# Expert layers of a transformer-like kernel: four of 32 token tiles taken unsorted through all eight experts

## The chip, the cores and the metric

The kernel runs on one core of one Trainium2 chip, in one launch. The metric is the device time in microseconds; lower is better. Engines are TensorE (PE, with its weight loads as PEld), VectorE (DVE), ScalarE (ACT), GpSimd (POOL) and SyncE (SP), which here only starts DMAs.

## The reference, cut to what matters

The input is 4 x 1024 tokens of 128 numbers, float32. Four layers follow each other, each as x = x + layer(layernorm(x)): an attention, a mixture of experts, a delta-rule attention, and the mixture of experts again. The change touches the two expert layers alone, which use the same weights:

```python
x = hidden_states.reshape(-1, H)                 # 4096 rows of 128
probs = softmax(x @ gate_w)                      # 8 experts
top_w, top_i = top_k(probs, 2)
top_w = top_w / sum(top_w)
route = zeros((m, E)); route[row, top_i] = top_w
for e in range(E):                               # 8 experts, F = 256
    h = silu(x @ w1[e]) * (x @ w3[e])            # 128 -> 256, twice
    out = out + route[:, e:e+1] * (h @ w2[e])    # 256 -> 128
```

A row thus needs two of the eight experts.

## The kernel before

All of x lies in on-chip memory as 32 tiles (`NT`) of 128 rows; the weights of all experts lie in `wall` (`all_w_all` in the trace). `moe` is one expert layer; it is called twice ("moe1", whose output the next layer norm reads, and "moe2", whose output is the kernel's). Each engine has its own instruction list, and they meet at semaphores; nothing is reordered by a scheduler. A layer has four stages.

**Planning.** VectorE finds the two best experts of each row (`find_best`), marks the row's pair of experts among 28 (`PAIRS`; `count_pairs` writes `member` and its sum `chosen`), and TensorE sums `chosen` over lanes (`before`, `total`, semaphore `s_pos`). From these, `pair_totals` works out where each pair begins; `experts_of_tiles` works out which experts each sorted tile needs; `places` gives each row its slot in the sorted order (`slot`); `order_passes` and `read_plan` turn it into a list of passes, which the engines later read into registers. ScalarE meanwhile writes the normalised rows into `xr`, with the row's weights behind them.

**Scatter.** When `slot` is there, GpSimd starts one indirect DMA per tile, 32 in all, which write the rows of `xr` to DRAM in sorted order (`expert_rows`). When all have landed, SyncE loads the sorted tiles back (`moe_moe_xs`).

**Passes.** Sorted by pairs, a tile needs few experts. There are `NPASS` = 2 * 32 + 27 = 91 passes of one tile through one expert. A pass is `up` (four 128x128 products into `ps_up`, weights from a copy `wbuf` that ScalarE makes), Silu on ScalarE, `product` on VectorE, `down` (two products into `ps_y`) and `add` on VectorE. TensorE runs `up(n)` and then `down(n - 2)`, and turns a sorted tile every second pass (`turn_rows`, into `ps_g`; VectorE copies it to `xgT`).

**Return.** For each sorted tile whose passes are done, GpSimd starts an indirect DMA that adds the tile's rows to the copy of x in DRAM (`rows_and_out` in moe1, the output itself in moe2). In moe1 SyncE then loads x back in four pieces, and VectorE takes each tile's statistics (`bn_stats_of`) for the next layer norm.

A float32 product of 128 moving columns or of 512 stands in the trace as two records, a turned tile as one.

## Time and profile before

| | us |
|---|---|
| median of 3 runs | 1899.91 (1897.85 to 1900.02) |
| the profiled execution | 1899.49 |
| its span, first to last instruction | 1897.8 |
| mean granted TensorE clock, share of full speed | 0.824 |
| moe1, from its first instruction to the last statistics | 863.8 to 1074.4 |
| moe2, from its first instruction to the end | 1694.9 to 1897.8 |

Starts are counted from the first instruction of the span. "PEclk" is the granted clock in a stretch as a share of full speed: 0.50 is 1.2 GHz and 1.00 is 2.4 GHz. The two expert layers are 413 us of the span. Over the whole span PE is busy 67% of the time and DVE 76%, but these are means over stages with different limits, so what matters here is read from the stages of one expert layer.

### The profile page before, as it was taken

Reading aid. Unit: us, or ns where it says so; the run is one execution under the profiler, and the core shown is the slowest. Engines: PE = TensorE matmul, PEld = TensorE weight load, DVE = VectorE, ACT = ScalarE, POOL = GpSimd, SP = SyncE. Lnnn points to the kernel's source line nnn. Section 1 sums busy time; section 2 is a strip of 40 time slices with the busy share of each in tenths; the row PEclk is TensorE's granted clock in tenths of the full one; section 3 lists DMA queues with packets and bytes.
Section 4 is the critical chain, followed back from the end, with each engine's and each line's share of the span. In section 5 each row is a group of like instructions: output and inputs, shape, how many; then the busy total and the mean of one; then the engine's idle time right before and its main releaser. Section 6 shows DMA issues by size and latency. Waiting matters only on the chain. (4 is left out here: it accounts for less than half of the span.)

```text
span 1897.8 us, 41781 instructions
## 1 busy us (share of the span) xinstructions
PE 1272.3 (67%) x15730; PEld 780.1 (41%) x15730; DVE 1438.5 (76%) x2659; ACT 963.9 (51%) x2025; POOL 327.9 (17%) x408
## 2 busy tenths in 40 slices
PE   4689999999999999992499483000000039950998
PEld 2214555555555555452499342000000014430997
DVE  4698989999989999515265485999999979871564
ACT  4607888888888888874266372000222200021565
POOL 6100000000000000004325200000000025546055
PEclk9859999999999999995699785555555569985999
DMA  3520111111111110022312326810222110011222
GB/s 94 171 55 9 41 42 32 31 31 31 31 31 31 31 31 3 3 67 64 82 12 26 56 94 125 208 45 11 52 54 63 40 50 0 1 45 48 54 23 25
DMA packets 100857, 92.14 MB, mean 49 GB/s; under 512 B 20977, under 2 KB 82226, under 8 KB 100274
## 3 DMA queue, kind: packets, MB, share of 16 engines
q1 hardware_dynamic: 83778, 76.08, 15.4%
q0 software_dynamic: 11264, 8.92, 3.3%
q10 hardware_dynamic: 5616, 4.47, 1.4%
q8 instruction: 127, 2.08, 0.5%
q14 instruction: 72, 0.59, 0.1%
HBM read 47.28 MB, written 31.21 MB: 41 GB/s over the span
## 5 line engine op out<-in xcount | busy, mean ns | idle before, releaser
L727 DVE TENSOR_REDUCE att_negmax<-att_ps_max 128x1 f32<-128x1024 f32 x512 | 621.0, 1224 | 66.7 <-PE att_ps_max L590 38.0
L715 ACT ACTIVATE att_probs<-att_ps_prob 128x512 f32<-128x512 f32 x1024 | 556.4, 595 | 129.4 <-PE att_ps_prob L605 127.2
L590 PE MATMUL att_ps_max<-av_k_op,av_q_op 81*32 81x512 bf16 x4096 | 423.1, 401 | 13.2 <-PEq L104 7.2
L605 PE MATMUL att_ps_prob<-av_q_op,av_k_op 99*32 99x512 bf16 x4096 | 412.3, 382 | 2.8
L625 PE MATMUL att_ps_acc<-att_probs,att_vq 128*32 128x256 f32 x4096 | 317.7, 379 | 0.0
L1960 PE MATMUL out_ps_y<-all_bo_row,all_ones 1*128 1x128 f32 x2 | 0.8, 481 | 372.7 <-PEq L104 372.7
L1123 PE MATMUL moe_moe_ps_up<-moe_moe_xgT,moe_moe_wbuf 128*128 x1456 | 196.6, 279 | 0.0
L1123 PEld LDWEIGHTS moe_moe_ps_up<-moe_moe_xgT,moe_moe_wbuf 128*128 128x128 f32 x1456 | 181.4, 196 | 0.1
L590 PEld LDWEIGHTS att_ps_max<-av_k_op,av_q_op 81*32 81x32 bf16 x4096 | 117.0, 97 | 142.6 <-DVE att_negmax L727 44.7
L605 PEld LDWEIGHTS att_ps_prob<-av_q_op,av_k_op 99*32 99x32 bf16 x4096 | 108.8, 95 | 146.2 <-ACT att_probs L715 88.7
L625 PEld LDWEIGHTS att_ps_acc<-att_probs,att_vq 128*32 128x32 f32 x4096 | 135.5, 111 | 75.6 <-issue 1.0
L1181 ACT ACTIVATE moe_moe_gate<-moe_moe_ps_up 128x256 f32<-128x256 f32 x182 | 70.0, 385 | 165.9 <-PE moe_moe_ps_up L1123 159.0
L1960 PEld LDWEIGHTS out_ps_y<-all_bo_row,all_ones 1*128 1x128 f32 x2 | 0.5, 304 | 372.9 <-issue 372.9
L1862 ACT ACTIVATE solve_p<-solve_state,solve_decay 128x32 f32<-128x32 f32 x128 | 45.0, 352 | 155.6 <-DVE solve_state L1846 155.6
L1173 ACT ACTIVATE moe_moe_wbuf<-all_w_all 128x512 f32 x182 | 113.3, 622 | 14.5 <-issue 14.4
L1131 PE MATMUL moe_moe_ps_y<-all_w_all,moe_moe_hT 128*128 x728 | 111.5, 276 | 1.3 <-DVE moe_moe_y L1337 1.3
L1337 DVE SCALAR_TENSOR_TENSOR moe_moe_y<-moe_moe_ps_y,moe_moe_xs,moe_moe_y 128x128 f32 x182 | 63.9, 351 | 62.8 <-issue 60.4
L1328 DVE TENSOR_TENSOR moe_moe_hT<-moe_moe_gate,moe_moe_ps_up 128x256 f32<-128x256 f32 x182 | 76.7, 421 | 43.2 <-PE moe_moe_ps_y L1131 31.8
L531 POOL CAST att_nm_parts<-att_nm_rows 32x128 bf16<-32x128 f32 x16 | 4.6, 286 | 547.2 <-ACT att_nm_rows L696 547.2
L1131 PEld LDWEIGHTS moe_moe_ps_y<-all_w_all,moe_moe_hT 128*128 128x128 f32 x728 | 96.1, 192 | 2.1 <-issue 2.1
L1955 POOL TENSOR_TENSOR out_qS<-b_q,out_St 128x1024 f32<-128x1024 f32 x32 | 75.4, 2355 | 65.8 <-DVE out_St L2064 65.8
L1323 DVE COPY moe_moe_xgT<-moe_moe_ps_g 128x128 f32<-128x128 f32 x64 | 18.2, 284 | 82.0 <-issue 80.7
(276 smaller groups left out, 1737.2 us busy)
## 6 DMA issues: line engine op xcount, KB each, us to landing
av_k_op<-terms_k SPq DMA_DIRECT2D x48, 216.0 KB
av_q_op<-terms_q SPq DMA_DIRECT2D x144, 72.0 KB
solve_dec_and_windows<-solve_Xw SPq DMA_DIRECT2D x16, 256.0 KB, 3.0
solve_dec_and_windows<-solve_k SPq DMA_DIRECT2D x16, 256.0 KB, 3.7
moe_moe_xs<-expert_rows SPq DMA_DIRECT2D x6, 576.0 KB, 6.6
terms_q<-qkv_parts_q SPq DMA_DIRECT2D x8, 384.0 KB, 2.6
terms_k<-qkv_parts_k SPq DMA_DIRECT2D x8, 384.0 KB, 3.1
all_w_all<-in_f_w SPq DMA_DIRECT2D x24, 128.0 KB, 2.4
```

Source lines behind the costliest of these rows:

```text
L590: mm = pe.matmul(ps_max[c * STRIP:(c + 1) * STRIP, a % 2, k * CH:(k + 1) * CH], q_op[s][0:R_ALL, h, at:at + STRIP], k_op[s][0:R_ALL, h, k ...
L605: mm = pe.matmul(ps_prob[c * STRIP:(c + 1) * STRIP, j % 2, :], k_op[s][0:R_END, h, at:at + STRIP], q_op[s][0:R_END, h, half * CH:(half + 1 ...
L625: mm = pe.matmul(ps_acc[half][32 * h:32 * h + 32, cols], vq[:, s % 2, kt, VW * h:VW * h + 32], probs[:, (GH * v + h) % PROBS, cols], start ...
L715: act.activation(probs[:, j % PROBS, :], ps_prob[:, j % 2, :], ACT.Exp).then_inc(s_exp, 1)
L727: dve.tensor_reduce(negmax[:, s % 2, a:a + 1], ps_max[:, a % 2, :], AX.X, ALU.max, negate=True).then_inc(s_maxed, 1)
L1123: mm = pe.matmul(ps_up[n % 3][:, i * P:(i + 1) * P], wbuf[:, n % 3, i * P:(i + 1) * P], xgT[:, bass.ds(row, P)], start=True, stop=True)
L1131: mm = pe.matmul(ps_y[n % 2][:, 0:P], hT[:, n % 3, i * P:(i + 1) * P], wall[:, bass.ds(at0 + (2 * F + i * P), P)], start=(i == 0), stop=(i ...
L1173: act.activation(wbuf[:, n % 3, :], wall[:, bass.ds(at0, 2 * F)], ACT.Copy).then_inc(s_wb, 1)
L1181: act.activation(gate[:, n % 3, :], ps_up[n % 3][:, 0:F], ACT.Silu).then_inc(s_silu, 1)
L1328: dve.tensor_tensor(hT[:, n % 3, :], gate[:, n % 3, :], ps_up[n % 3][:, F:2 * F], ALU.mult).then_inc(s_h, 1)
L1337: dve.scalar_tensor_tensor(out=tile, in0=ps_y[n % 2][:, 0:P], scalar=xs_flat[:, bass.ds(col, 1)], in1=tile, op0=ALU.mult, op1=ALU.add).the ...
L1955: pool.tensor_tensor(qS[:, e % 2, :], q[:, b * S:(b + 1) * S], St[:, e % 2, :], ALU.mult).then_inc(s_qS, 1)
```

## The change

The first four tiles of x (`ND`, 512 rows) are no longer sorted, scattered and returned. TensorE turns them to `xdT`, and they go through all eight experts as they lie, 512 rows at a time: for each expert `first_up` twice (two products of 512 columns each, into four `ps_up` banks), `first_silu`, `first_product`, `first_down` (eight products of 128 columns) and `first_sum`, which adds the weighted result into `y_d`. A weight of zero makes an expert that a row doesn't need drop out. This work stands in the instruction lists between the planning steps and ahead of the passes. The other 28 tiles (`NS`) are sorted as before, so that there are 28 scatters, 2 * 28 + 27 = 83 passes and 28 returns. `places` stands ahead of `experts_of_tiles`. ScalarE's normalisations are spread between the Silus, and each scatter waits for its own tile's piece (`PIECE`, four tiles) instead of for all. In moe1 the DRAM copy of x is laid out with the 32 rows of a lane behind each other, so that a lane's share of a load or store is one run; it comes back in pieces of seven tiles instead of eight. In moe2 SyncE stores the four tiles by itself.

```diff
-NPASS = 2 * NT + PAIRS - 1
+ND = 4
+NS = NT - ND
+NPASS = 2 * NS + PAIRS - 1
 COL_W, COL_ID, COL_ZERO, ROW = P, P + E, P + 12, 144
 PIECE = 4
 NPIECE = NT // PIECE
-PARTS = [0, 1, 2, 4, 8, 16, 24, 32]
-BACK = 8
+PARTS = [0, 1, 2, 4, 8, 16, 22, NS]
+BACK = 7
...
+        xdT = m.sb("xdT", [P, CH])
+        gate_d = m.sb("gate_d", [P, 2, CH])
+        hT_d = m.sb("hT_d", [P, 2, MF, CH])
+        y_d = m.sb("y_d", [P, ND, P])
...
-        ps_up = [m.ps(f"ps_up{i}", [P, 2 * F]) for i in range(3)]
+        ps_up = [m.ps(f"ps_up{i}", [P, 2 * F]) for i in range(4)]
...
-        resid_tiles = resid.rearrange("(t p) c -> p t c", p=P)
-        landed = 16 * NT * (layer + 1)
+        resid_tiles = resid.rearrange("(p t) c -> p t c" if out is None else "(t p) c -> p t c", p=P)
+        per_tile, per_lane = (1, NT) if out is None else (P, 1)
+        landed = 16 * NS * (layer + 1)
...
-            sp.dma_start(resid_tiles, g.x[:, :, :]).then_inc(s_kept, 16)
+            sp.dma_start(resid_tiles[:, ND:, :], g.x[:, ND:, :]).then_inc(s_kept, 16)
...
+            if not norm_next:
+                sp.wait_ge(s_dadd, 1)
+                sp.dma_start(resid_tiles[:, 0:ND, :], g.x[:, 0:ND, :]).then_inc(s_dout, 16)
...
+                for i in range(NS // BACK):
+                    some = slice(ND + i * BACK, ND + (i + 1) * BACK)
...
+            pool.iota(xr[:, :, COL_ID:COL_ID + 1].bitcast(mybir.dt.int32), pattern=[[per_tile, NT], [0, 1]],
+                      base=0, channel_multiplier=per_lane).then_inc(s_ids, 1)
...
-            pool.wait_ge(s_xn, NPIECE)
             pool.wait_ge(s_weight, 1)
             pool.wait_ge(s_slot, 1)
-            for t in range(NT):
-                pool.indirect_dma_start(scr.xg, bass.IndirectOffsetOnAxis(slot[:, t:t + 1], 0), xr[:, t, :],
+            for t in range(NS):
+                pool.wait_ge(s_xn, (ND + t) // PIECE + 1)
+                pool.indirect_dma_start(scr.xg, bass.IndirectOffsetOnAxis(slot[:, t:t + 1], 0), xr[:, ND + t, :],
                                         None).then_inc(s_scat, 16)
...
+            def first_up(u):
+                e, i = u // MF, u % MF
+                wait_used(pe, s_dh, u - 1)
+                for half in range(2):
+                    at0 = e * WE + half * F + i * P
+                    mm = pe.matmul(ps_up[(2 * u + half) % 4][:, :], wall[:, at0:at0 + P], xdT[:, :],
+                                   start=True, stop=True)
+                mm.then_inc(s_dup, 1)
+
+            def first_down(e):
+                pe.wait_ge(s_dh, MF * (e + 1))
+                wait_used(pe, s_dsum, e - 1)
+                for t in range(ND):
+                    for i in range(MF):
+                        at0 = e * WE + 2 * F + i * P
+                        mm = pe.matmul(ps_y[e % 2][:, t * P:(t + 1) * P], hT_d[:, e % 2, i, t * P:(t + 1) * P],
+                                       wall[:, at0:at0 + P], start=(i == 0), stop=(i == MF - 1))
+                mm.then_inc(s_dy, 1)
+
+            pe.wait_ge(s_xn, 1)
+            for t in range(ND):
+                mm = pe.transpose(ps_g[:, t * P:(t + 1) * P], xr[:, t, 0:P], g.ident[:, :])
+            mm.then_inc(s_dturn, 1)
+            pe.wait_ge(g.s_experts, 16 * 3 * E)
+            pe.wait_ge(s_dT, 1)
+            first_up(0)
+            first_up(1)
             pe.wait_ge(s_earlier, 2)
             pe.wait_ge(s_chosen, 1)
             pe.matmul(before, earlier[:, :], chosen[:, :], start=True, stop=True)
             pe.matmul(total, g.ones[:, :], chosen[:, :], start=True, stop=True).then_inc(s_pos, 1)
-            pe.wait_ge(s_count, 1)
-            pe.matmul(ps_prefix, earlier[:, :], local[:, E - 1:E], start=True, stop=True).then_inc(s_prefix, 1)
-            pe.wait_ge(s_turns, 1)
-            pe.wait_ge(s_tables, 9)
-            for e in range(E):
-                pe.matmul(ps_row, tile_b[:, :], turn_of[:, e, :], start=(e == 0), stop=(e == E - 1))
-            for e in range(E):
-                mm = pe.matmul(ps_exp, exp_b[:, e:e + 1], turn_of[:, e, :], start=(e == 0), stop=(e == E - 1))
-            mm.then_inc(s_passes, 1)
+            for e in range(1, E):
+                first_up(2 * e)
+                first_up(2 * e + 1)
+                first_down(e - 1)
+                if e == 1:
+                    pe.wait_ge(s_count, 1)
+                    pe.matmul(ps_prefix, earlier[:, :], local[:, E - 1:E], start=True, stop=True).then_inc(s_prefix, 1)
+                if e == 2:
+                    pe.wait_ge(s_turns, 1)
+                    pe.wait_ge(s_tables, 9)
+                    for j in range(E):
+                        pe.matmul(ps_row, tile_b[:, :], turn_of[:, j, :], start=(j == 0), stop=(j == E - 1))
+                    for j in range(E):
+                        mm = pe.matmul(ps_exp, exp_b[:, j:j + 1], turn_of[:, j, :], start=(j == 0), stop=(j == E - 1))
+                    mm.then_inc(s_passes, 1)
+            first_down(E - 1)
...
+                if n == 0:
+                    pe.wait_ge(s_dsum, E)
...
+            def normalise(q):
                 for tile in range(q * PIECE, (q + 1) * PIECE):
                     op = act.activation(xr[:, tile, 0:P], g.x[:, tile, :], ACT.Identity,
                                         bias=g.nmr[:, tile:tile + 1], scale=g.rstd[:, tile:tile + 1])
                 op.then_inc(s_xn, 1)
-                if q == 2:
-                    act.wait_ge(s_gap, 1)
-                    act.activation(tanh[:, :, :], gap[:, :, :], ACT.Tanh, scale=0.5).then_inc(s_tanh, 1)
+
+            def first_silu(e):
+                for u in (2 * e, 2 * e + 1):
+                    act.wait_ge(s_dup, u + 1)
+                    wait_used(act, s_dh, u - 1)
+                    act.activation(gate_d[:, u % 2, :], ps_up[2 * u % 4][:, :], ACT.Silu).then_inc(s_dsilu, 1)
+
+            normalise(0)
+            normalise(1)
+            act.wait_ge(s_dturn, 1)
+            act.activation(xdT[:, :], ps_g[:, :], ACT.Copy).then_inc(s_dT, 1)
+            normalise(2)
+            act.wait_ge(s_gap, 1)
+            act.activation(tanh[:, :, :], gap[:, :, :], ACT.Tanh, scale=0.5).then_inc(s_tanh, 1)
+            first_silu(0)
+            normalise(3)
+            normalise(4)
+            for e in range(1, E):
+                first_silu(e)
+                if 4 + e < NPIECE:
+                    normalise(4 + e)
...
+            places()
+
+            def first_product(u):
+                dve.wait_ge(s_dsilu, u + 1)
+                wait_used(dve, s_dy, u // MF - 1)
+                dve.tensor_tensor(hT_d[:, u // MF % 2, u % MF, :], gate_d[:, u % 2, :],
+                                  ps_up[(2 * u + 1) % 4][:, :], ALU.mult).then_inc(s_dh, 1)
+
+            def first_sum(e):
+                dve.wait_ge(s_dy, e + 1)
+                wait_used(dve, s_dsum, e)
+                for t in range(ND):
+                    weight = xr[:, t, COL_W + e:COL_W + e + 1]
+                    part_y = ps_y[e % 2][:, t * P:(t + 1) * P]
+                    if e == 0:
+                        op = dve.tensor_scalar(y_d[:, t, :], part_y, weight, None, ALU.mult)
+                    else:
+                        op = dve.scalar_tensor_tensor(out=y_d[:, t, :], in0=part_y, scalar=weight, in1=y_d[:, t, :],
+                                                      op0=ALU.mult, op1=ALU.add)
+                op.then_inc(s_dsum, 1)
+
+            first_product(0)
+            first_product(1)
             experts_of_tiles()
-            places()
-            order_passes()
-            read_plan()
+            dve.wait_ge(s_weight, 1)
+            for e in range(1, E):
+                first_product(2 * e)
+                first_product(2 * e + 1)
+                first_sum(e - 1)
+                if e == 1:
+                    order_passes()
+                if e == 3:
+                    read_plan()
+            first_sum(E - 1)
+            dve.wait_ge(s_dsum, E)
+            dve.wait_ge(s_xn, 1)
+            dve.tensor_tensor(g.x[:, 0:ND, :], g.x[:, 0:ND, :], y_d[:, :, :], ALU.add).then_inc(s_dadd, 1)
+            if norm_next:
+                dve.wait_ge(s_dadd, 1)
+                for t in range(ND):
+                    bn_stats_of(nc, g, t)
...
-                for i in range(NT // BACK):
+                for i in range(NS // BACK):
                     dve.wait_ge(s_home[i], 16)
-                    for t in range(i * BACK, (i + 1) * BACK):
+                    for t in range(ND + i * BACK, ND + (i + 1) * BACK):
```

TensorE's list at the start of moe1 (`ps_p` holds the planning's small products, `ps_g` the turned tiles) was this before, up to the first pass:

```order
L1102 MATMUL moe_moe_ps_p<-moe_moe_chosen,moe_moe_earlier 128x28
L1103 MATMUL moe_moe_ps_p<-moe_moe_chosen,all_ones 128x28
L1105 MATMUL moe_moe_ps_p<-moe_moe_local,moe_moe_earlier 128x1
L1109 MATMUL moe_moe_ps_p<-moe_moe_turn_of,moe_moe_tile_b 1x128 x8
L1111 MATMUL moe_moe_ps_p<-moe_moe_turn_of,moe_moe_exp_b 1x128 x8
L891 TENSOR_LOAD moe_moe_pe_at
L1116 MATMUL moe_moe_ps_g<-all_ident,moe_moe_xs 128x128 x2
L1123 ISA
L1123 MATMUL moe_moe_ps_up<-moe_moe_xgT,moe_moe_wbuf 128x128 x4
```

With the change the same place begins so (L1126 is `first_up`, L1136 `first_down`):

```order
L1142 MATMUL moe_moe_ps_g<-all_ident,moe_moe_xr 128x128 x4
L1126 MATMUL moe_moe_ps_up<-moe_moe_xdT,all_w_all 128x512 x4
L1150 MATMUL moe_moe_ps_p<-moe_moe_chosen,moe_moe_earlier 128x28
L1151 MATMUL moe_moe_ps_p<-moe_moe_chosen,all_ones 128x28
L1126 MATMUL moe_moe_ps_up<-moe_moe_xdT,all_w_all 128x512 x4
L1136 MATMUL moe_moe_ps_y<-all_w_all,moe_moe_hT_d 128x128 x8
L1158 MATMUL moe_moe_ps_p<-moe_moe_local,moe_moe_earlier 128x1
L1126 MATMUL moe_moe_ps_up<-moe_moe_xdT,all_w_all 128x512 x4
L1136 MATMUL moe_moe_ps_y<-all_w_all,moe_moe_hT_d 128x128 x8
L1163 MATMUL moe_moe_ps_p<-moe_moe_turn_of,moe_moe_tile_b 1x128 x8
```

Four products of 512 columns and their turns now stand ahead of the two sums over `chosen` on which the slots depend, and the remaining planning products stand between the experts. Thirty-two products of 512 columns and 64 of 128 stand ahead of the first `TENSOR_LOAD` of a pass.

VectorE's list from `chosen` on was this before (`place` to `slot` are `places`, `upper` to `local` are `experts_of_tiles`):

```order
L1247 TENSOR_REDUCE moe_moe_chosen<-moe_moe_member 128x28
...
L1262 TENSOR_TENSOR moe_moe_member<-moe_moe_base,moe_moe_ps_p 128x28
L1266 TENSOR_SCALAR moe_moe_upper<-moe_moe_ends,moe_moe_tile_to 128x28
...
L1273 SCALAR_TENSOR_TENSOR moe_moe_local<-moe_moe_unit,moe_moe_needed 128x8
L1278 SCALAR_TENSOR_TENSOR moe_moe_place<-moe_moe_carry,moe_moe_member 128x924
L1282 TENSOR_TENSOR moe_moe_picked<-moe_moe_member,moe_moe_place 128x896
L1283 TENSOR_REDUCE moe_moe_slot_f<-moe_moe_picked 128x32
L1284 TENSOR_SCALAR moe_moe_slot<-moe_moe_slot_f 128x32
```

and is this now; the last rows are what stands between the last expert and the first sorted tile:

```order
L1353 SCALAR_TENSOR_TENSOR moe_moe_place<-moe_moe_carry,moe_moe_member 128x812
L1357 TENSOR_TENSOR moe_moe_picked<-moe_moe_member,moe_moe_place 128x784
L1358 TENSOR_REDUCE moe_moe_slot_f<-moe_moe_picked 128x28
L1359 TENSOR_SCALAR moe_moe_slot<-moe_moe_slot_f 128x28
L1395 TENSOR_TENSOR moe_moe_hT_d<-moe_moe_gate_d,moe_moe_ps_up 128x512 x2
L1341 TENSOR_SCALAR moe_moe_upper<-moe_moe_ends,moe_moe_tile_to 128x28
...
L1407 SCALAR_TENSOR_TENSOR moe_moe_y_d<-moe_moe_ps_y,moe_moe_xr,moe_moe_y_d 128x128 x8
L1426 TENSOR_TENSOR all_x<-all_x,moe_moe_y_d 128x512
L215 BN_STATS all_stats<-all_x 128x6 x4
L1435 COPY moe_moe_xgT<-moe_moe_ps_g 128x128 x2
```

The slots no longer stand behind the six steps of `experts_of_tiles`, and the first `xgT` copy, for which the first pass waits, stands behind the sums of the last two experts, the addition to x and (in moe1) four statistics.

## Rows read from the trace of the kernel before

**Rows 1.** The profile page, first line

```profile
span 1897.8 us, 41781 instructions
```

**Rows 2.** Busy time of stretches of moe1: PE, PEld, DVE, ACT, POOL, PEclk, DMA

```profile
884.00:926.00 42.00, 1.87 (x16) 1.58 (x16) 2.19 (x10) 3.17 (x4) 31.49 (x32) 0.50 0.16 56
928.00:935.00 7.00, 6.29 (x28) 5.96 (x29) 1.63 (x5) 1.81 (x4) 0.00 (x0) 0.50 0.97 181
935.00:1059.00 124.00, 123.13 (x1098) 122.57 (x1097) 74.61 (x208) 78.82 (x175) 47.62 (x31) 1.00 0.22 26
```

**Rows 3.** Timeline of the passes: start, duration, engine, line, operation, idle time before

```profile
941.05 0.27 PE L1116 MATMUL moe_moe_ps_g<-all_ident,moe_moe_xs 128*128 128x128 f32 x1
...
1045.84 1.06 PE L1123 MATMUL moe_moe_ps_up<-moe_moe_xgT,moe_moe_wbuf 128*128 x8
...
1055.21 1.06 PE L1123 MATMUL moe_moe_ps_up<-moe_moe_xgT,moe_moe_wbuf 128*128 x8
```

**Rows 4.** Timeline of moe1's planning

```profile
868.20 4.73 ACT L1165 ACTIVATE moe_moe_xr<-all_x,all_nmr,all_rstd 128x128 f32<-128x128 f32 x12 [1.57 <-DVE all_nmr L1215]
...
873.47 1.09 DVE L1247 TENSOR_REDUCE moe_moe_chosen<-moe_moe_member 128x28 f32<-128x896 f32 x1
...
874.70 0.60 PE L1102 MATMUL moe_moe_ps_p<-moe_moe_chosen,moe_moe_earlier 128*128 128x28 f32 x2 [11.95 <-DVE moe_moe_chosen L1247]
...
875.83 0.20 DVE L1260 TENSOR_TENSOR_SCAN moe_moe_ends<-moe_moe_unit,moe_moe_ps_p 128x28 f32<-128x28 f32 x1
...
876.39 0.23 DVE L1266 TENSOR_SCALAR moe_moe_upper<-moe_moe_ends,moe_moe_tile_to 128x28 f32<-128x28 f32 x1
...
877.96 2.07 DVE L1278 TENSOR_TENSOR_SCAN moe_moe_place<-moe_moe_carry,moe_moe_member 128x924 f32<-128x924 f32 x1
...
882.88 0.18 DVE L1284 TENSOR_SCALAR moe_moe_slot<-moe_moe_slot_f 128x32 uint32<-128x32 f32 x1
```

**Rows 5.** Timeline of moe1: first and last scatter, first sorted tile, first pass

```profile
883.99 1.70 POOL L1088 DMA_INDIRECT expert_rows<-moe_moe_xr,moe_moe_slot  x1 [12.11 <-DVE moe_moe_slot L1284]
...
923.97 0.96 POOL L1088 DMA_INDIRECT expert_rows<-moe_moe_xr,moe_moe_slot  x1 [0.31 <-issue]
...
928.13 0.47 PE L1116 MATMUL moe_moe_ps_g<-all_ident,moe_moe_xs 128*128 128x128 f32 x1 [41.57 <-DMA moe_moe_xs<-expert_rows]
...
929.42 2.06 PE L1123 MATMUL moe_moe_ps_up<-moe_moe_xgT,moe_moe_wbuf 128*128 x8
```

**Rows 6.** Timeline of moe2: its first pass

```profile
1760.39 2.05 PE L1123 MATMUL moe_moe_ps_up<-moe_moe_xgT,moe_moe_wbuf 128*128 x8
```

**Rows 7.** Timeline of the delta-rule output stage, products of 512 columns

```profile
1545.60 5.65 PE L1968 MATMUL out_ps_k<-b_k,out_spread 128*128 128x512 f32 x8 [7.49 <-DVE out_gather L2035]
1553.12 1.98 PE L1968 MATMUL out_ps_k<-b_k,out_spread 128*128 128x512 f32 x4 [1.88 <-DVE out_St L2064]
...
1560.81 1.88 PE L1968 MATMUL out_ps_k<-b_k,out_spread 128*128 128x512 f32 x4
1562.53 1.89 PE L1978 MATMUL out_ps_o<-out_qS,out_gather 128*128 128x512 f32 x4
```

**Rows 8.** Groups by line, whole span: busy us, mean ns, idle before

```profile
L804 ACT ACTIVATE oproj_xT<-oproj_ps_x 128x512 f32<-128x512 f32 x8 | 4.7, 593 | 3.9 <-PE oproj_ps_x L833 3.9
L868 DVE TENSOR_TENSOR all_x<-all_x,oproj_ps_y 128x512 f32<-128x512 f32 x8 | 5.5, 686 | 8.2 <-PE oproj_ps_y L825 8.2
L1337 DVE SCALAR_TENSOR_TENSOR moe_moe_y<-moe_moe_ps_y,moe_moe_xs,moe_moe_y 128x128 f32 x182 | 63.9, 351 | 62.8 <-issue 60.4 <-DVE moe_moe_y L1337 1.3 <-PE moe_moe_ps_y L1131 1.1
```

**Rows 9.** Timeline of moe1's return: loads of x, statistics

```profile
1063.32 3.97 SPq L1047 DMA_DIRECT2D all_x<-rows_and_out  x4
1067.53 1.65 DVE L215 BATCH_NORM_STATS2 all_stats<-all_x 128x6 f32<-128x128 f32 x8 [8.11 <-DMA all_x<-rows_and_out]
...
1071.14 3.30 DVE L215 BATCH_NORM_STATS2 all_stats<-all_x 128x6 f32<-128x128 f32 x16 [0.16 <-DMA all_x<-rows_and_out]
```

**Rows 10.** One group by tile, the returns of moe1: min/median/max ns, first and last start

```profile
L1095 POOL DMA_INDIRECT rows_and_out<-moe_moe_y,moe_moe_ids x32: 1554/1556/1617, 976.7 to 1060.0; - x32
```

69 lines of the change are left out of this document (37 added, 32 removed).

## The prediction

> **What bounds the kernel now.** The span is 1897.8 us [rows 1] and the profiled execution took 1899.49 us, 0.4 us under the median of 1899.91; the sum is made against the execution. I read the busy times by stage first. While the rows are scattered, TensorE is busy 1.87 of 42 us, VectorE 2.19 and ScalarE 3.17; GpSimd has 31.49 us in 32 scatters. In the passes TensorE is busy 123.13 of 124 us at 2.4 GHz (PEclk 1.00), the others two thirds at most [rows 2]. So a layer is a stage bound by the count of scatters, with TensorE idle, and then one bound by the count of passes on TensorE. The timeline gives the rates. From 1045.84 to 1055.21 seven passes start, 1.339 us apart; each record in a pass is thus about 0.112 us (twelve a pass), and each turned tile adds one more record [rows 3]. The scatters start at 883.99 and 923.97, so 1.265 us apart after the longer first; the first sorted tile is turned 4.16 us after the last of them starts, and the first pass starts 1.29 us later, at 929.42 [rows 5]. In moe2 the first pass is at 1760.39 [rows 6], 830.97 us later, and I treat both layers alike but for the return.
>
> **Fewer passes.** Eight passes less are 8 x 1.339 = 10.7 us, four turned tiles less 4 x 0.112 = 0.4: 11.2 us less on each layer (with the roundings), on the path, since TensorE never rests there.
>
> **When the slots come.** ScalarE normalises at 0.394 us a tile from 868.20 (twelve in 4.73) [rows 4]. The first four tiles are there at 869.8, turned by about 871.8; ScalarE has done its eight tiles at 871.4 and copies `xdT` in 0.59 us [rows 8], so `first_up` starts near 872.6, from a cold clock. Eight records of 512 columns that started after 7.49 us of idleness took 5.65 us where at full clock they take 8 x 0.43 = 3.44 (four of them stand 1.72 us apart) [rows 7]. That is what two `first_up` cost: until 878.3. `chosen` is done at 874.56, and its sums start now at 874.70 [rows 4]; with the change they queue behind until 878.3, 3.6 us later. VectorE has nothing else to do ahead of `pair_totals`. From there `slot` took 883.06 - 875.83 = 7.23 us; without `experts_of_tiles` (876.39 to 877.96) that is 5.66, and 28 tiles instead of 32 cut an eighth of the 4.92 us between `place` and `slot` [rows 4], so 5.1. The slots come at 875.83 + 3.6 + 5.1 = 884.5, not earlier but 1.5 us later than before.
>
> **When the sorted rows are there.** Twenty-eight scatters end 4 x 1.265 = 5.1 us sooner. The pieces of `xr` that each waits for are ready: ScalarE's Silus (0.59 us) and four normalisations (1.6 us) fit in what TensorE needs for an expert. The first sorted tile could be turned at 928.13 + 1.5 - 5.1 = 924.5 and a first pass start at 925.8, 3.6 us sooner than 929.42, if nothing else held it.
>
> **When the first four tiles are done.** TensorE stands in `first_up(2)` until `first_product(0)`, which VectorE reaches after `slot`: 884.5 + 0.69 [rows 8] + 0.1 = 885.3. Left then are 14 `first_up` of 1.72 us, 24.1; eight `first_down` of 16 records at 0.112, 14.3; the planning's small products, at most the 1.87 us that they are busy now at the low clock [rows 2], 1.2; and a restart at 1.2 GHz after 6 us of idleness, 5.65 - 3.44 = 2.2 by the same row. Sum 41.8, end at 927.1. Nothing else is slower: for one expert TensorE needs 5.2 us, VectorE two products (1.37) and four sums (1.4), ScalarE 2.8, and every buffer has a second one. Behind the last product VectorE has four sums (4 x 0.351, or nearer 1.3), the addition to x (0.69), in moe1 four statistics at 0.206 us (16 in 3.30 [rows 9]), a copy of 0.3 and waits of some 0.2. So the first pass starts at 930.4 in moe1, 1.0 us later than before, and 0.8 sooner, 0.2 us later than before, in moe2. This and not the rows (925.8) decides. Its bounds: 925.8 if the clock and the small products cost nothing, and 3 us later if a turned expert costs 0.35 us more in waits.
>
> **The clock at the first pass.** Before, TensorE comes from 42 idle us and runs at 0.50 until 935 [rows 2], 5.6 us that cost 2.8. Now it rests only some 3 us between `first_down(7)` and the first pass. After 1.88 us of idleness four records of 512 still took 1.98 us, as in the steady run [rows 7], after 7.49 they did not; 3 us lies between. Ends: the whole 2.8 us a layer is gained, or nothing. I take 1.2 a layer.
>
> **The return of moe1.** Now the first statistics start 4.2 us after the loads, and the others follow at 1.81 us for eight tiles, where eight statistics take 1.65, so the DMAs set the pace and the end is at 1074.44 [rows 9]. With 28 tiles it is at worst 1.58 us a piece, 0.7 us less in all. The longer runs may land faster, and then 28 statistics at 0.206 us behind a first piece that comes up to 1 us sooner give 2.1 us less. I take 1.5. The return of the last tile in moe2 stays.
>
> **Sum.** moe1: +1.0 - 11.2 - 1.2 - 1.5 = -12.9. moe2: +0.2 - 11.2 - 1.2 = -12.2. Together -25.1: 1899.5 - 25.1 = 1874.4 us. All ends to the good: first passes at 3.6 us sooner, 2.8 of clock a layer, 2.1 of return: -7.2 - 22.4 - 5.6 - 2.1 = -37.3, 1862. All ends to the bad: first passes 3 us later than forecast, no clock, 0.7 of return: +7.2 - 22.4 - 0.7 = -15.9, 1884.
>
> **Rivals.** *Scatters slowed by VectorE.* Now VectorE is idle while GpSimd scatters; with the change it works through all of it. If a scatter then took what a return takes, 1.56 us [rows 10] instead of 0.96, the sorted rows would come 28 x 0.6 = 16.6 us later, the first pass at 942.4; +13.0 - 11.2, no clock gain, is +1.8 a layer, and 1901.5 in all after the return's 1.5. It decides only beyond 930.4 - 925.8 = 4.6 us, 0.16 us a scatter. Against it: the 32 returns take between 1554 and 1617 ns each, the last ones with VectorE idle and the rest with it busy 60% of the time [rows 2, 10], so that their cost is their own. Chance 0.06.
>
> The Trainium skill has the rule for it (SBUF — State Buffer, section "SBUF: two separate sides"): GpSimd and VectorE share a pair of ports, and while VectorE runs a two-port operation GpSimd can't write the descriptors of its DMAs. By that rule only such operations count, and of the new ones the sums and products read one operand from PSUM, so by it the sum would stay at 1874.4, where a rule for every operation of VectorE would give the 1901.5; the returns' even times agree, but no row here has a scatter beside such an operation.
>
> *The first tiles never reach the pace of the rows of 512.* It is one mechanism: TensorE waits at each expert for VectorE's products, rests, and stays at 1.2 GHz; then the 38.4 us of products take 76.8, the first pass is 36 us later, and the kernel is at 1874.4 + 72 = 1946, slower. It decides from 12 us more a layer, that is from 1.5 us of waiting an expert. Against it: rows 7 show the same shapes at full clock with VectorE in between, and the chain Silu, product (1.3 us and latencies) is shorter than the `first_up` (1.72 us) that covers it. Chance 0.05.
>
> *The rows decide, and the clock holds.* The first tiles are done at 925.8 or sooner and the clock stays up: -3.6 - 11.2 - 2.8 a layer and -1.5, 1862.8. It needs a restart without the 2.2 us, which rows 7 speak against. Chance 0.06.
>
> **How the numbers follow.** My forecast, with its range of 1863 to 1884, has 0.83, the rivals 0.17 with a little left for a stall that I don't see. A time within 0.2% of before, 3.8 us, is about what a measurement can't tell from no change; only a partly slowed scatter lies there, 0.03. Slower has 0.06: the second rival and part of the first. Faster has 0.91. The range of 1863 to 1886 leaves out the two first rivals and the far edge of the third.
>
> **What would show it.** In the changed trace: the sums over `chosen` start near 878.3 and `slot` ends near 884.5; 28 scatters 1.265 us apart; PEclk 0.50 at the start of `first_up(2)` and 1.00 within some 4 us; the last `first_down` ends near 927 and the first pass of moe1 starts near 930.4; passes at 1.34 us; the first statistics of moe1's return under 4.2 us after the loads. The prediction is wrong if a scatter takes over 1.45 us, if PE is idle inside the 40 us from `first_up(2)` to the last `first_down` by more than 3 us, or if the first pass starts after 935.

## The result and the profile after

| | us |
|---|---|
| the changed kernel, median of 4 runs | 1913.91 (1912.78 to 1915.88) |
| the kernel before, median of 4 runs | 1899.13 (1897.85 to 1900.02) |
| ratio | 1.0076, 95% interval 1.0063 to 1.0088 |
| span of the profiled execution, before and after | 1897.8 and 1914.1 |

It is slower by 14.8 us; forecast was 1874.4. Rows of before are named by their group ahead of the prediction; the line numbers are those of the changed kernel (L1126 `first_up`, L1136 `first_down`, L1230 `first_silu`, L1222 `normalise`, L1395 `first_product`, L1407 `first_sum`, L1109 the scatter, L1172 `turn_rows`, L1179 `up`).

First I looked for the first pass. TensorE's timeline of the changed kernel, moe1:

```profile
940.36 3.73 PE L1136 MATMUL moe_moe_ps_y<-all_w_all,moe_moe_hT_d 128*128 128x128 f32 x32
943.93 0.27 PE L1172 MATMUL moe_moe_ps_g<-all_ident,moe_moe_xs 128*128 128x128 f32 x1
947.23 0.44 PE L1172 MATMUL moe_moe_ps_g<-all_ident,moe_moe_xs 128*128 128x128 f32 x1 [3.03 <-DVE moe_moe_xgT L1435]
947.47 2.06 PE L1179 MATMUL moe_moe_ps_up<-moe_moe_xgT,moe_moe_wbuf 128*128 x8
...
949.53 3.62 PE L1179 MATMUL moe_moe_ps_up<-moe_moe_xgT,moe_moe_wbuf 128*128 x16
```

The first pass starts at 947.47, where it was at 929.42 [rows 5] and 930.4 was forecast. `first_down(7)` is still running at 943, so the delay arose in the first tiles' work. That stretch had to be read, engine by engine, from the last point at which all was on time. TensorE, then ScalarE, VectorE and GpSimd, all of the changed kernel in moe1:

```profile
895.05 1.95 PE L1136 MATMUL moe_moe_ps_y<-all_w_all,moe_moe_hT_d 128*128 128x128 f32 x16
...
897.91 3.70 PE L1126 MATMUL moe_moe_ps_up<-moe_moe_xdT,all_w_all 128*128 128x512 f32 x8
901.45 0.76 PE L1136 MATMUL moe_moe_ps_y<-all_w_all,moe_moe_hT_d 128*128 128x128 f32 x3
902.65 0.60 PE L1136 MATMUL moe_moe_ps_y<-all_w_all,moe_moe_hT_d 128*128 128x128 f32 x3 [0.44 <-issue]
904.06 0.27 PE L1136 MATMUL moe_moe_ps_y<-all_w_all,moe_moe_hT_d 128*128 128x128 f32 x1 [0.81 <-issue]
...
911.16 0.37 PE L1136 MATMUL moe_moe_ps_y<-all_w_all,moe_moe_hT_d 128*128 128x128 f32 x1 [0.84 <-issue]
919.67 2.07 PE L1126 MATMUL moe_moe_ps_up<-moe_moe_xdT,all_w_all 128*128 128x512 f32 x2 [8.14 <-DVE moe_moe_hT_d L1395]
```
```profile
896.11 1.34 ACT L1230 ACTIVATE moe_moe_gate_d<-moe_moe_ps_up 128x512 f32<-128x512 f32 x2 [4.18 <-PE moe_moe_ps_up L1126]
897.35 1.64 ACT L1222 ACTIVATE moe_moe_xr<-all_x,all_nmr,all_rstd 128x128 f32<-128x128 f32 x4
918.30 1.09 ACT L1230 ACTIVATE moe_moe_gate_d<-moe_moe_ps_up 128x512 f32<-128x512 f32 x2 [19.31 <-remote]
```
```profile
896.74 1.43 DVE L1395 TENSOR_TENSOR moe_moe_hT_d<-moe_moe_gate_d,moe_moe_ps_up 128x512 f32<-128x512 f32 x2 [1.51 <-ACT moe_moe_gate_d L1230]
904.79 1.13 DVE L1407 SCALAR_TENSOR_TENSOR moe_moe_y_d<-moe_moe_ps_y,moe_moe_xr,moe_moe_y_d 128x128 f32<-128x128 f32 x4 [6.62 <-remote]
918.93 1.28 DVE L1395 TENSOR_TENSOR moe_moe_hT_d<-moe_moe_gate_d,moe_moe_ps_up 128x512 f32<-128x512 f32 x2 [13.01 <-ACT moe_moe_gate_d L1230]
```
```profile
914.06 0.96 POOL L1109 DMA_INDIRECT expert_rows<-moe_moe_xr,moe_moe_slot  x1 [0.30 <-issue]
921.18 0.96 POOL L1109 DMA_INDIRECT expert_rows<-moe_moe_xr,moe_moe_slot  x1 [6.16 <-ACT moe_moe_xr L1222]
...
924.97 0.96 POOL L1109 DMA_INDIRECT expert_rows<-moe_moe_xr,moe_moe_slot  x1 [0.30 <-issue]
```

Until some 893 us all goes nearly as forecast; the Silu at 896.11 comes 2.6 us after `first_up(4)` ended (893.50). Then ScalarE idles 19.31 us ahead of the Silu of `first_up(6)`, whose records begin at 897.91 and whose last one had ended by 899.90. VectorE idles 6.62 us ahead of the sum of `first_down(1)`, which TensorE had ended at 897.0. TensorE gets through `first_down(2)` in 10 us where the one before took 1.95. "Remote" means that the trace shows the signal, but no instruction that ended just before it. The trace also records when a semaphore goes up (a signal, that is), and this is what names the fault: the signal of `first_down(0)` is recorded 0.9 us after its last record ended, that of `first_down(1)` at 904.77, 7.8 us after; that of `first_up(6)` at 918.27, 18.4 us after; those of `first_up(7)`, of the small products and of `first_down(2)` between 918.2 and 918.5. ScalarE's and VectorE's signals that it records come 0.01 us after their instruction; many of theirs are missing from the record here, but the engine that waits goes on at once (the Silu ended at 897.45, its product starts at 897.48; h1 below shows the same inside a stall). **TensorE's signals, and not ScalarE's or VectorE's, come up to 20 us late**, and the last of them come some 3 us after GpSimd has stopped (914.06 + 0.96; it waits for rows that ScalarE, stuck in the Silu, has not normalised). From 926 on a `first_down` is again 5.22 us after the last, and every signal is prompt. moe2 does the same at the same place (ScalarE; the Silu waits for `first_up(6)`, whose signal is recorded at 1759.72, 18.5 us after it ended, so the DMA in the brackets is a wrong guess of the view):

```profile
1738.33 0.60 ACT L1230 ACTIVATE moe_moe_gate_d<-moe_moe_ps_up 128x512 f32<-128x512 f32 x1 [0.88 <-DMA moe_moe_xs<-expert_rows]
...
1759.74 1.08 ACT L1230 ACTIVATE moe_moe_gate_d<-moe_moe_ps_up 128x512 f32<-128x512 f32 x2 [19.29 <-DMA moe_moe_xs<-expert_rows]
```

The windows of the changed kernel, as in [rows 2]:

```profile
884.00:926.00 42.00, 28.15 (x110) 16.31 (x110) 13.14 (x39) 9.26 (x20) 27.85 (x28) 0.74 0.14 48
928.00:935.00 7.00, 7.00 (x29) 4.07 (x28) 3.18 (x7) 1.79 (x3) 0.00 (x0) 1.00 0.88 173
935.00:1059.00 124.00, 120.97 (x1033) 118.64 (x1032) 72.42 (x203) 75.09 (x164) 37.42 (x24) 0.97 0.17 21
```

While the rows are scattered TensorE is busy 28.15 of 42 us at 0.74 of full clock; without the stall (g0, below) it is 40.95 at 0.97.

### The profile page after: what moved, and what is told of

It reads as the page before. It is cut to its first block and busy times, and to the rows that moved or that the text cites. A ratio compares the mean times of both kernels' runs of the same rounds, so it can differ in the third digit from the quotient of the medians.

```text
span 1914.1 us, 42049 instructions
## 1 busy us (share of the span) xinstructions
PE 1351.9 (71%) x15922; PEld 817.0 (43%) x15922; DVE 1463.3 (76%) x2717; ACT 969.3 (51%) x2027; POOL 307.2 (16%) x392
## 5 line engine op out<-in xcount | busy, mean ns | idle before, releaser
L727 DVE TENSOR_REDUCE att_negmax<-att_ps_max 128x1 f32<-128x1024 f32 x512 | 621.1, 1223 | 67.1 <-PE att_ps_max L590 38.0
L1179 PE MATMUL moe_moe_ps_up<-moe_moe_xgT,moe_moe_wbuf 128*128 x1328 | 179.5, 280 | 0.0
L1179 PEld LDWEIGHTS moe_moe_ps_up<-moe_moe_xgT,moe_moe_wbuf 128*128 128x128 f32 x1328 | 165.3, 196 | 0.3
L1256 ACT ACTIVATE moe_moe_gate<-moe_moe_ps_up 128x256 f32<-128x256 f32 x166 | 63.8, 384 | 91.8 <-PE moe_moe_ps_up L1179 87.0
L1248 ACT ACTIVATE moe_moe_wbuf<-all_w_all 128x512 f32 x166 | 103.3, 622 | 0.5 <-issue 0.3
L1189 PE MATMUL moe_moe_ps_y<-all_w_all,moe_moe_hT 128*128 x664 | 101.9, 276 | 1.3 <-DVE moe_moe_y L1449 1.3
L1449 DVE SCALAR_TENSOR_TENSOR moe_moe_y<-moe_moe_ps_y,moe_moe_xs,moe_moe_y 128x128 f32 x166 | 58.2, 351 | 58.1 <-issue 55.6
L1440 DVE TENSOR_TENSOR moe_moe_hT<-moe_moe_gate,moe_moe_ps_up 128x256 f32<-128x256 f32 x166 | 69.9, 421 | 39.7 <-PE moe_moe_ps_y L1189 25.5
L1126 PE MATMUL moe_moe_ps_up<-moe_moe_xdT,all_w_all 128*128 128x512 f32 x128 | 71.1, 703 | 26.6 <-DVE moe_moe_hT_d L1395 24.2
L1189 PEld LDWEIGHTS moe_moe_ps_y<-all_w_all,moe_moe_hT 128*128 128x128 f32 x664 | 87.8, 193 | 2.1 <-issue 2.1
```

Of the source, the lines that this page charges most:

```text
L727: dve.tensor_reduce(negmax[:, s % 2, a:a + 1], ps_max[:, a % 2, :], AX.X, ALU.max, negate=True).then_inc(s_maxed, 1)
L1126: mm = pe.matmul(ps_up[(2 * u + half) % 4][:, :], wall[:, at0:at0 + P], xdT[:, :], start=True, stop=True)
L1179: mm = pe.matmul(ps_up[n % 3][:, i * P:(i + 1) * P], wbuf[:, n % 3, i * P:(i + 1) * P], xgT[:, bass.ds(row, P)], start=True, stop=True)
L1189: mm = pe.matmul(ps_y[n % 2][:, 0:P], hT[:, n % 3, i * P:(i + 1) * P], wall[:, bass.ds(at0 + (2 * F + i * P), P)], start=(i == 0), stop=(i ...
L1248: act.activation(wbuf[:, n % 3, :], wall[:, bass.ds(at0, 2 * F)], ACT.Copy).then_inc(s_wb, 1)
L1256: act.activation(gate[:, n % 3, :], ps_up[n % 3][:, 0:F], ACT.Silu).then_inc(s_silu, 1)
```

## Experiments

These theories could explain the stall:

- A: the planning's small products, which now run among scatters (L1163, L1165), set it off.
- B: it is the scatters, 1.265 us apart, beside TensorE's work. B1: what counts is their rate. B2: how long they go on. B3: the number of TensorE's instructions.
- C: the long comparison `turn_of`, which stretches one scatter.
- D: an order of waits between the three engines, with no part of the scatters.
- E: something in the first tiles' own data or order.
- F, which came later: the chip.

Kernels of a group ran on one chip, each group on another. A kernel with the small products behind the last `first_down` (e1_products_last), meant for theory A, gave no result; e3 and e4 test that theory in its place.

### Group I: where the stall goes when the scatters or the products move

**e2_scatter_last** holds the scatters back until the first tiles are done.

```diff
             pool.wait_ge(s_slot, 1)
+            pool.wait_ge(s_dsum, E)
             for t in range(NS):
```

> The changed kernel with GpSimd waiting for the last first_sum before its first scatter, so that no scatter lies beside the first tiles' products. All theories that lay the stall to the scatters (A, B, C): no stall, an expert each 5.22 us, last first_down at about 926.6, then 28 scatters of 1.265 us from 930 to 965.4, first pass at about 970: +22.5 us a layer, about 1959. If the stall comes of the order of waits of TensorE, ScalarE and VectorE alone (theory D), it is still there: last first_down at 940, first pass at 984, about 1987.

Measured: 1955.44 us in one run. There is no stall: from the third expert on a `first_down` starts every 5.22 us, the last at 920.88. D has fallen, since e3, in the same group, does stall.

**e3_scatter_after_products** has `pool.wait_ge(s_passes, 1)` in that place.

> The changed kernel with GpSimd waiting for the planning products (done at about 898) before its first scatter; 28 scatters from 898.2 to 933.6. Theory A (products among scatters) and theory C (turn_of among scatters): no stall, dense work ends at about 927, first pass 5.4 us after the last scatter starts (932.4), at 937.8: 9.7 us earlier a layer than in the changed kernel, about 1894.5. Theory B (some 13 us of back-to-back scatters): the stall comes again 13 us after the first scatter, at about 911, and lasts till some 3 us after the last one, 936.5, with about three experts left: first pass at about 955, about 1929.

Measured: 1921.74 us (1920.82 to 1924.44), ratio 1.012 (1.0104 to 1.0137). ScalarE in moe1, whose first scatter starts at 899.37 and whose last at 933.70:

```profile
905.52 0.60 ACT L1231 ACTIVATE moe_moe_gate_d<-moe_moe_ps_up 128x512 f32<-128x512 f32 x1 [1.38 <-issue]
907.24 0.60 ACT L1231 ACTIVATE moe_moe_gate_d<-moe_moe_ps_up 128x512 f32<-128x512 f32 x1 [1.12 <-PE moe_moe_ps_up L1127]
916.41 0.60 ACT L1231 ACTIVATE moe_moe_gate_d<-moe_moe_ps_up 128x512 f32<-128x512 f32 x1 [8.57 <-remote]
921.28 0.60 ACT L1231 ACTIVATE moe_moe_gate_d<-moe_moe_ps_up 128x512 f32<-128x512 f32 x1 [4.28 <-remote]
938.92 1.09 ACT L1231 ACTIVATE moe_moe_gate_d<-moe_moe_ps_up 128x512 f32<-128x512 f32 x2 [17.04 <-remote]
```

The stall has moved with the scatters, though neither products nor `turn_of` lie among them: A and C have fallen, B stands.

**e4_products_at_5** moves the products to expert 5 and `read_plan` to expert 6 (`if e == 5`, `if e == 6`).

> The changed kernel with the planning products in the turn of expert 5 and read_plan in that of expert 6. Theory A: the stall moves with the products, from 899 to about 914, and ends when GpSimd pauses (last scatter 919.5, so about 923): last first_down at about 935, first pass at about 942, 5.5 us earlier a layer, about 1903. Theories B and C: the stall stays at 899 to 918, about 1914.

Measured: 1915.89 us in one run; the Silu of `first_up(6)` starts at 905.89 and that of `first_up(8)` at 922.89, with the products still to come. The stall stays about where it was: A fell here too.

### Group II: wider scatters, and work that nobody needs

**e5_paced** has GpSimd clear some columns of a spare tile behind each scatter, to keep scatters apart.

```diff
                 pool.indirect_dma_start(scr.xg, bass.IndirectOffsetOnAxis(slot[:, t:t + 1], 0), xr[:, ND + t, :],
                                         None).then_inc(s_scat, 16)
+                pool.memset(idle[:, 0:128 if layer == 0 else 320], 0.0).then_inc(s_idle, 1)
+                pool.wait_ge(s_idle, t + 1)
```

> The changed kernel with a small clearing on GpSimd behind each scatter: 128 columns in the first expert layer (period about 1.55 us where it was 1.265), 320 columns in the second (about 1.75 us). Theory B1 (TensorE's signals pile up because GpSimd's scatters and TensorE's work together outrun something; it is a matter of rate): lateness shrinks or goes with the wider period. Without any stall the last scatter starts at 927 in the first layer and the first pass at about 933 (947.5 in the changed kernel), in the second layer 9 us earlier than in the changed kernel: about 1891. Theory B2 (any stretch of scatters over some 10 us jams TensorE's signals, however spaced): the stall lasts until 3 us after the last scatter, first pass later than in the changed kernel by some 5 us a layer: about 1925.

Measured: 1882.56 us (1880.98 to 1883.93), ratio 0.9912 (0.9895 to 0.9928). No signal is late; from first scatter to first pass it takes 45.3 us in moe1 and 49.9 in moe2.

**e6_wide_or_tied** clears 576 columns in moe1; in moe2 it has `pool.wait_ge(s_dup, t // 2 + 2)` ahead of each scatter in place of the clearing.

> The changed kernel; first expert layer: a clearing of 576 columns on GpSimd behind each scatter (period about 2.0 us, last scatter starts at about 938); second: no clearing, but scatter t waits for first_up number t/2 + 2, so that GpSimd stops by itself while TensorE's signals are late. Theory B1: first layer no stall, first pass at about 944 (set by the rows), 3.5 us earlier than in the changed kernel; second layer: last scatter and last first_down together, about 43 us after the first scatter, first pass some 14 us earlier than in the changed kernel: about 1897. Theory B2: the first layer stalls to the end of the scatters, first pass about 955 or later; the second layer, whose scatters pause for less than 1 us at a time, stalls as well: 1915 or more.

Measured: 1887.63 us (1884.99 to 1888.42), ratio 0.9933 (0.9915 to 0.995). No stall in either layer; in moe1 the rows decide, with a first pass at 939.66.

**e7_fill_f32** is the kernel before with this on TensorE beside the scatters, and one small copy on ScalarE for each signal:

```diff
+            for k in range(18):
+                for i in range(2 if layer == 0 else 4):
+                    cols = 2 * F if layer == 0 else P
+                    mm = pe.matmul(ps_up[(2 * k + i) % 3][:, 0:cols], g.ident[:, :], wall[:, 0:cols],
+                                   start=True, stop=True)
+                mm.then_inc(s_fill, 1)
```

> The kernel before the change with work on TensorE that nobody needs beside its 32 scatters: 18 groups of matmuls, each signalled to ScalarE, which makes one small copy for each. First expert layer: two matmuls of 512 columns in float32 a group (0.43 us each record); second: four of 128 columns (0.11 us each record). Theory B: the copies of ScalarE fall behind the matmuls by several us some 7 to 13 us after the first scatter, in both layers. If the number of TensorE's instructions a us is what counts (B3), the second layer falls behind sooner and by more; if only the time since the first scatter counts, both at the same place. Theory E (the stall needs the first tiles' own data or order): no lateness. Time: some us over the kernel before if the fill ends late, else the same.

**e8_fill_bf16_or_sparse** has 24 groups of six bf16 products in moe1, and 24 single products, each after the copy of the one before, in moe2.

> As the run before, with other fill: first expert layer 24 groups of six bf16 matmuls of 512 columns (one pass of 0.21 to 0.43 us each), second: 24 times one float32 matmul of 128 columns, each of which waits for ScalarE's copy of the one before, so that TensorE is idle nearly all the time and the round trip is seen. B3 (number of TensorE's instructions counts): little or no lateness in the sparse layer, a round trip of about 1 us throughout. B2 (scatters alone jam TensorE's signals): the round trip grows to several us from about 7 us after the first scatter in the sparse layer too.

Measured: 1899.81 and 1899.28 us, one run each, and no copy is late (1.72, 0.89, 1.30 and 1.30 us apart to the end). Taken by themselves these two said that TensorE's work isn't enough. But one thing in the traces did not fit: a layer's scatters raise their semaphore 16 times each, and in this group the trace has nearly all of these increments (448 of 448 in e5, 512 of 512 in e7), while that of the changed kernel has 167 and 165 of 448 in its two layers, and e3's 103 and 94. The chip might be the difference. So nothing of this group could be held against group I without the changed kernel beside it.

### Group III: the changed kernel again, and the pace that works

> The changed kernel itself, beside the others of this group on the same chip, since the runs without lateness were made on another chip than those with it. Theory B1 (the stall is one of rate, on any chip): stall as before in both layers, first_silu(3) 19 us late, about 1914. Theory F (the stall belongs to the chip of those runs): none here, about 1877.

Measured (**c0_after_again**, the changed kernel itself): 1915.35 us (1912.95 to 1916.98), ratio 1.0076 (1.0059 to 1.0093); the Silu of `first_up(6)` at 918.13, 182 and 179 of 448 increments in the trace.

**b1_paced_both** clears 128 columns in both layers.

> The changed kernel with a clearing of 128 columns on GpSimd behind each scatter in both expert layers (period 1.50 us). Theory B1: no lateness, the first pass 45.3 us after the first scatter in both layers (49.9 in the second layer of the run with 320 columns there): 1882.6 - 4.6 = 1878, 36 us under the changed kernel on the same chip. Theory F: no difference to the changed kernel but for the wider period, which hardly matters while the dense work ends last: both about 1878.

Measured: **1880.26 us (1877.35 to 1881.63), ratio 0.9898 (0.9881 to 0.9914)**, 35 us under the changed kernel on the same chip. GpSimd, ScalarE and TensorE of this kernel in moe1 (its L1111 is the scatter, L1234 the Silu, L1140 `first_down`, L1176 `turn_rows`, L1183 `up`):

```profile
895.66 0.97 POOL L1111 DMA_INDIRECT expert_rows<-moe_moe_xr,moe_moe_slot  x1 [0.28 <-POOL moe_moe_idle L1113]
896.63 0.22 POOL L1113 MEMSET moe_moe_idle<- 128x128 f32 x1
897.13 0.97 POOL L1111 DMA_INDIRECT expert_rows<-moe_moe_xr,moe_moe_slot  x1 [0.28 <-issue]
```
```profile
899.95 0.60 ACT L1234 ACTIVATE moe_moe_gate_d<-moe_moe_ps_up 128x512 f32<-128x512 f32 x1 [2.55 <-PE moe_moe_ps_up L1130]
...
905.17 0.60 ACT L1234 ACTIVATE moe_moe_gate_d<-moe_moe_ps_up 128x512 f32<-128x512 f32 x1 [1.37 <-issue]
906.89 0.60 ACT L1234 ACTIVATE moe_moe_gate_d<-moe_moe_ps_up 128x512 f32<-128x512 f32 x1 [1.12 <-issue]
```
```profile
901.47 1.95 PE L1140 MATMUL moe_moe_ps_y<-all_w_all,moe_moe_hT_d 128*128 128x128 f32 x16
...
906.69 1.95 PE L1140 MATMUL moe_moe_ps_y<-all_w_all,moe_moe_hT_d 128*128 128x128 f32 x16
...
929.16 0.48 PE L1176 MATMUL moe_moe_ps_g<-all_ident,moe_moe_xs 128*128 128x128 f32 x1 [3.08 <-DMA moe_moe_xs<-expert_rows]
...
930.45 2.06 PE L1183 MATMUL moe_moe_ps_up<-moe_moe_xgT,moe_moe_wbuf 128*128 x8
```

The Silu of `first_up(6)` starts at 899.95 where it was 918.30, and the first pass at 930.45. Here the sorted rows, which the wider scatters bring later, decide the first pass: TensorE is done with the first tiles at 926.1 and waits 3.08 us for the rows. 1.265 us from scatter to scatter stalls, 1.46 (the median) doesn't. (This trace has 259 and 277 of 448 increments: lost records alone are no stall.)

**a3_small_silu_or_pace1**: in moe1 `first_silu` over 128 columns from u = 4 on; in moe2 a clearing of one column.

> First expert layer: the changed kernel, with first_silu over 128 of 512 columns from the third group on (the outputs are then not those of the reference), so ScalarE works a quarter as long. Second layer: a clearing of one column behind each scatter (period about 1.38 us by a 0.10 us clearing). If ScalarE's work is part of what jams, the first layer's stall shortens or goes; if not, first_silu(3) is 19 us late as before. In the second layer theory B1 gives a shorter stall or none, if the limit lies under 1.38 us; with none the layer is 18 us shorter.

**a2_rows_first**: in moe1 all `normalise` ahead of the third Silu; in moe2 `first_product` over 128 columns from u = 4 on.

> First expert layer: the changed kernel with all rows normalised ahead of the third first_silu, so that GpSimd never waits for ScalarE and its scatters run on to the end. Theory B1: the stall then ends some 3 us after the last scatter, at about 923, not at 918.3: 4 us worse than the changed kernel. Second layer: the rows as in the changed kernel, first_product over 128 of 512 columns from the third group on (the outputs are then not those of the reference): if VectorE's work is part of what jams, the stall there shortens or goes; if not, it stays as in the changed kernel.

Measured: 1911.38 and 1918.70 us, one run each. From first scatter to first pass c0 needs 63.9 us in moe1 and 63.2 in moe2. A small Silu leaves 63.9, a small product 62.4: with a quarter of ScalarE's or of VectorE's load in these steps the stall stays. All rows first makes 67.1, 3.3 more, about as expected: GpSimd no longer pauses, and the stall lasts until it has ended. One column (28 scatters in 37.5 us, 1.35 apart at the median) gives 58.9, against 45.2 in b1: a shorter stall. GpSimd clears and waits for itself here too, so it is the distance that helps and not the clearing. So the rate counts, B1, and for this work the bound lies between 1.35 and 1.46 us.

### Group IV: the control does not stall

> The changed kernel again, as the control of this group on its chip: first_silu(3) 19 us late in both layers, about 1914, on whatever chip.

**g0_after_control**, the changed kernel again, took **1879.03 us** where the kernel before took 1901.47, one run each. Its page's first line, and ScalarE in moe1:

```profile
span 1877.3 us, 42049 instructions
```
```profile
898.71 0.60 ACT L1230 ACTIVATE moe_moe_gate_d<-moe_moe_ps_up 128x512 f32<-128x512 f32 x1 [2.55 <-PE moe_moe_ps_up L1126]
900.43 0.60 ACT L1230 ACTIVATE moe_moe_gate_d<-moe_moe_ps_up 128x512 f32<-128x512 f32 x1 [1.12 <-PE moe_moe_ps_up L1126]
```

The scatters are as dense as ever (first 883.70, last 918.21), all 448 increments are in the trace in both layers, and no signal is late. The expectation was wrong and theory F right: the same program stalls on one chip and not on another.

> The kernel before with TensorE's fill alone (512 columns in the first expert layer, 128 in the second), once more, now beside the control. If it shows no lateness again (copies of ScalarE 0.9 to 1.7 us apart to the end) while the control stalls, TensorE's work and the scatters alone do not make the stall. If the copies now fall behind by several us, the chip made the difference, and any stream of TensorE does it.

> The kernel before with a chain like that of the first tiles beside its 32 scatters: a group is two matmuls of 512 columns, a Silu of 512 columns on ScalarE, a product of 512 columns on VectorE, and TensorE waits for the product of two groups before; in the second expert layer each group has four small matmuls of 128 columns too. If the three engines' traffic with the scatters makes the stall, it shows in both layers from about 8 us after the first scatter; if the small matmuls or TensorE's instructions a us are needed, only in the second; if neither shows it, the stall hangs on something of the first tiles that this leaves out (weights and rows that change, waits across two experts, the sums).

> The changed kernel with, from the second expert on, one of the four sums of first_sum (both layers) and, in the second expert layer alone, one of the four tiles of first_down too (8 of 32 records; the outputs are then not those of the reference). If VectorE's sums matter the first layer's stall shortens or goes; if TensorE's small matmuls matter, the second layer's goes while the first layer's stays. If neither matters both layers stall 19 us, about 1914 less some us for the shorter second layer.

Measured, one run each: **g2_fill_again** (e7 again) 1895.88, **g1_fill_chain** 1903.94, **a1_fewer_sums** 1866.26 us, and nothing late in any. On a chip whose control does not stall they tell nothing about the stall.

### Group V: the control stalls, and so do two streams of work that nobody needs

> The changed kernel, control of this group. On a chip whose trace records all increments: 1879 us, ratio to the kernel before 0.988 to 0.99. On one whose trace loses more than half of them: 1914 to 1915, ratio 1.0076. Anything between would speak against a tie of the stall to the chip.

> The kernel before with the chain of three engines beside its scatters. If the control stalls and the stall needs only that three engines work beside scatters 1.265 us apart, some Silu of the chain starts several us late in both layers; where the control does not stall, 1.7 us apart all along, as on the chip before.

> The kernel before with TensorE's fill alone. If the control stalls and TensorE's stream alone is enough, the copies of ScalarE fall behind here too, more so in the second layer with its short matmuls; if the stall needs ScalarE's and VectorE's part, no copy is late. Where the control does not stall: no copy is late.

Measured: **h0_after_third**, the control, 1915.76 us (1912.23 to 1918.46), ratio 1.0097 (1.008 to 1.0114), 168 and 149 of 448 increments in the trace. **h1_chain_again** 1933.39 us and **h2_fill_third** 1908.63, one run each, where the same two programs took 1903.94 and 1895.88 in group IV. ScalarE's copies of the fill in moe2, here and then in g2_fill_again (first scatter at 1716.12 here, last at 1755.98):

```profile
1722.96 0.20 ACT L1185 ACTIVATE moe_moe_gate<-all_ident 128x1 f32<-128x1 f32 x1 [0.69 <-issue]
1725.19 0.20 ACT L1185 ACTIVATE moe_moe_gate<-all_ident 128x1 f32<-128x1 f32 x1 [2.02 <-PE moe_moe_ps_up L1120]
1728.73 0.20 ACT L1185 ACTIVATE moe_moe_gate<-all_ident 128x1 f32<-128x1 f32 x1 [3.34 <-PE moe_moe_ps_up L1120]
1735.09 0.20 ACT L1185 ACTIVATE moe_moe_gate<-all_ident 128x1 f32<-128x1 f32 x1 [6.16 <-remote]
1742.87 0.20 ACT L1185 ACTIVATE moe_moe_gate<-all_ident 128x1 f32<-128x1 f32 x1 [7.58 <-remote]
1761.07 0.20 ACT L1185 ACTIVATE moe_moe_gate<-all_ident 128x1 f32<-128x1 f32 x1 [18.00 <-remote]
```
```profile
1722.67 0.20 ACT L1185 ACTIVATE moe_moe_gate<-all_ident 128x1 f32<-128x1 f32 x1 [0.69 <-PE moe_moe_ps_up L1120]
1723.56 0.20 ACT L1185 ACTIVATE moe_moe_gate<-all_ident 128x1 f32<-128x1 f32 x1 [0.69 <-PE moe_moe_ps_up L1120]
1724.46 0.20 ACT L1185 ACTIVATE moe_moe_gate<-all_ident 128x1 f32<-128x1 f32 x1 [0.69 <-PE moe_moe_ps_up L1120]
```

TensorE's stream and the scatters are enough, so E has fallen too. With short products (128 columns) the first late copy is 9 us after the first scatter, with long ones (512, moe1) 20 us (902.39 after 881.92; this one by 0.2 us, the next by 4.2). That fits B3, the more instructions of TensorE a microsecond, the sooner. But the short products also signal more often, every 0.90 us against every 1.72, so that the rate of the signals explains it as well; no run here parts the two. With the long ones TensorE itself goes on undisturbed (its last record starts at 917.02), and only its signals wait, the last copy until 928.21; with the short ones it is slowed too.

h1 also shows whose signals are late inside a stall, since there each engine waits for another. ScalarE, VectorE and TensorE in moe1:

```profile
913.52 0.60 ACT L1193 ACTIVATE moe_moe_fgate<-moe_moe_ps_up 128x512 f32<-128x512 f32 x1 [6.39 <-remote]
914.15 0.69 DVE L1345 TENSOR_TENSOR moe_moe_fh<-moe_moe_fgate,moe_moe_ps_up 128x512 f32<-128x512 f32 x1 [6.30 <-issue]
914.89 3.68 PE L1124 MATMUL moe_moe_ps_up<-all_w_all 128*128 128x512 f32 x4 [5.00 <-issue]
```

TensorE had ended its part at 909.89, and the Silu starts 3.6 us later. VectorE starts 0.03 us after the Silu has ended, and TensorE 0.05 us after VectorE has.

## Why the prediction was wrong

**The step that failed** is "When the first four tiles are done": the sum of 41.8 us, end at 927.1, counted TensorE's instructions and the waits for data, and took it that a signal arrives when the instruction has ended; a late signal stood in it at nothing, without a reason. On the chip of the result the signals due between 898 and 911.5 us came in one heap at 918.2 to 918.5, and the last `first_down` ended near 944, 17 us late. The text had "a little left for a stall that I don't see"; it should have had much more, because no row of before had TensorE at work beside scatters 1.265 us apart. Between the two spans, from the traces of before and after:

| part | forecast | measured |
|---|---|---|
| first pass, moe1 | +1.0 | +18.05 (947.47 - 929.42) |
| passes of moe1, first `up` to last `add` | -11.2 - 1.2 | -11.03 |
| return of moe1, last return to last statistics | -1.5 | -1.8 |
| the layers between | 0 | +3.7 |
| first pass of moe2, from its first Sqrt | +0.2 | +19.6 |
| passes of moe2 | -11.2 - 1.2 | -11.45 |
| behind them | 0 | -0.6 |
| sum | -25.1 | +16.4 |

In g0, without the stalls, the rows are -1.2, -11.0, -1.8, +5.7, 0.0, -11.5 and -0.6: -20.5 us, a span of 1877.3. The stalls thus are 19.3 and 19.6 us. Two of the prediction's own signs of being wrong came: TensorE is idle inside the first tiles by far more than 3 us, and the first pass starts after 935.

- *Slot at 884.5*: measured 882.97. The two `first_up` from the cold clock held up VectorE's `ends` until 877.59, not until 879.4; from there it took 5.4 us, not 5.1. Too cautious by 1.5 us, and no matter.
- *Scatters 1.265 us apart*: right but for the first, the one beside `turn_of` and the pause in the stall. *Rows ready at 924.5, not deciding*: right where nothing stalls (in g0 the last scatter starts at 918.21, TensorE ends the last `first_down` at 924.8 and then waits 3.02 us for VectorE, and the first pass is at 928.21).
- *First pass 930.4*: right in kind and within 2.2 us in g0; 17 us off on the chip of the result. That b1 has 930.45 is luck: there the rows decide, not the first tiles.
- *Fewer passes 11.2*: measured 11.03 and 11.45.
- *1.2 us of clock a layer*: it did not come. The first `up` records of after are 2.06 us for eight, as at the low clock, though TensorE had rested 3 us only; of the two ends "nothing" was right.
- *Return -1.5*: -1.8. The first statistics start 3.83 us after the loads (1070.34 to 1074.17), and all 28 then follow without a wait in 5.51 us, as the second case had it.
- *Rival 1, slowed scatters*: wrong in its general form. 26 of moe1's 28 scatters take 0.95 to 0.98 us, most of them beside sums and products with an operand in PSUM; the first takes 1.18. But one is stretched to 1.74 us (1.90 in moe2), the one beside `turn_of`, a comparison whose two inputs and result lie in SBUF; in moe1 it ends 0.83 us after the comparison. So was the first of before, 1.70 [rows 5], beside the same comparison: the row that the prediction called missing was there. The Trainium skill (SBUF — State Buffer, section "SBUF: two separate sides") has an operation of VectorE with two SBUF inputs hold the shared ports against an operation of GpSimd that reads SBUF. The trace agrees for `turn_of`, if the scatter counts as such a read.
- *Rival 2, low clock throughout*: no. In g0 the granted clock is 0.97 of full speed from 884 to 926; in the result it fell again only in the stall, when TensorE had to wait (two records of 512 in 2.07 us at 919.67).
- *Small slips without effect*: 28 x 0.6 is 16.8, not 16.6, and the range's upper end is given as 1884 and as 1886. The result lies outside both.

**What the runs don't settle.** The tie to the chip rests on three runs of the changed kernel that stall (the result, c0, h0) and one that doesn't (g0, with three more kernels beside it, none of which stalls). Each chip was used on one occasion, so that chip and occasion can't be told apart. No run speaks against the tie to increments lost from the trace: every kernel that stalled had lost some, and on the two chips with nearly all of them (e7; g0 and its group) nothing stalled. The kernel before, too, lost them beside the first result, 271 of 512 recorded in moe1. Signals and trace records might share a path that is full sooner on some chips; this is argued, not shown. All times here are of executions that the profiler recorded, so whether an unrecorded one stalls too was not tried. Nor was e5 or b1 run beside the changed kernel on a chip without the stall: what the wider pace costs there is only bounded by 1880.3 against 1879.0 on different chips, and by a way from first scatter to first pass that is 1.0 and 0.2 us longer in b1 than in g0.

## What to carry to other kernels

A signal can be a cost of its own. Where one engine issues DMAs back to back for tens of microseconds, look in the trace whether the signals of the others still come when their instructions end; if they are late, spread the issues (0.20 us more between scatters bought 35 us here, on a chip that stalls). When a result hangs on such a stretch, put a control in each group of experiments, since two groups without one had me hold a chip's difference for a kernel's. And where "nothing ran beside this before" is the reason that no row shows a cost, the range must be wide on that side.

## What the hardware showed beyond that

**A loop in an untouched layer became slower.** The solver between the expert layers (VectorE) is the same code in both kernels; the rows are its first instruction after the loop turns, before and then after:

```profile
1422.48 0.49 DVE L1828 TENSOR_TENSOR solve_p<-solve_state,solve_dec_and_windows 128x128 f32<-128x128 f32 x2 [2.95 <-issue]
...
1478.32 0.49 DVE L1828 TENSOR_TENSOR solve_p<-solve_state,solve_dec_and_windows 128x128 f32<-128x128 f32 x2 [2.69 <-issue]
```
```profile
1429.61 0.49 DVE L1940 TENSOR_TENSOR solve_p<-solve_state,solve_dec_and_windows 128x128 f32<-128x128 f32 x2 [5.00 <-issue]
...
1487.48 0.49 DVE L1940 TENSOR_TENSOR solve_p<-solve_state,solve_dec_and_windows 128x128 f32<-128x128 f32 x2 [4.94 <-issue]
```

Both waits are longer, by 2.05 and 2.25 us. The runs tell what they hang on. They are 4.93 to 5.52 us in every kernel made from the changed one but a1, which has 21 sums fewer on VectorE ahead of the loop: 2.79 and 2.69. The kernel before with a fill on TensorE and copies on ScalarE (e7, e8, g2, h2) keeps 2.69 to 3.02, but with 18 products more on VectorE ahead of the loop (g1, h1) it has 4.93 to 5.19. So it is the length of VectorE's list ahead of the loop that decides. The queue of instruction packets shows three of 8 KB in 1415 to 1425 us before and four in 1420 to 1432 after. The Trainium skill has a reason (Runtime: NRT & Kernel Launch, section "Instruction fetch mechanics"): a taken branch to code outside the window that is held must fetch it first. The trace agrees as to the place, the turn of the loop; that the longer list moved the loop over such a bound is argued, not shown. The two waits are 4.3 us, more than the whole +3.7 of the table and most of the +5.7 of g0, and most of what g0 lacks to the forecast of 1874.4.

**The gate.** TensorE rested only 3.0 us (943.93 + 0.27 to 947.23) before the first pass, after 20 us of steady work at 2.4 GHz (granted clock 1.00 from 923 to 944), and its next records still ran at 1.2 GHz (eight in 2.06 us, then 16 in 3.62), up to 953.6. In [rows 7] a rest of 1.88 us had left it at full clock.
